# Two-layer graph network on one core: GpSimd makes the weighted one-hot columns of six of the 37 edge groups

## The chip, the cores and the metric

The kernel runs on one core of a Trainium2 chip. The metric is the device time of one execution in microseconds (us): the median of three timed runs. The engines are TensorE (PE in the profile, PEld for its weight loads), VectorE (DVE), ScalarE (ACT), GpSimd (POOL) and SyncE (SP, which here only issues DMAs).

## The reference, cut to what matters

There are N = 1250 nodes of F = 1024 features and E = 40000 edges, sorted by destination.

```python
h = jnp.maximum(_layernorm(x), 0.0)
W = jnp.zeros((1024, 1024)).at[src, dst].add(edge_weight)   # sparse weight matrix
x = x + h @ W.T + L0_bias
h = jnp.maximum(_layernorm(x), 0.0)
# two graph layers over the same edges
agg = segment_sum(h[src], dst); mean = agg / max(deg, 1)
h1 = relu(h @ W_self0 + mean @ W_neigh0 + b0)
out = x + (h1 @ W_self1 + mean(h1) @ W_neigh1 + b1)
```

Both uses of the edges are matrices that can be built once: the counts A (how many edges go from source s to destination d) and the weights W.

## The kernel before, in words

**The edge stage** builds A and W. The 40000 edges form NG = 40 groups of GC = 8 chunks with EP = 125 edges each, one edge on each partition. For each group j, VectorE makes three things in `group_rows(j)`:

- `R[:, j % 6]` (`hot_rows`, L1661): for each chunk 125x128 one-hot rows of the source's low bits, 1024 columns in bf16;
- the first part of `L[:, j % 6]` (`hot_keys`, L1668): one-hot columns of the destination, within a window of WDS[j] destinations times TN = 10 source tiles;
- the second part of `L` (`weigh`, L1676): three weighted copies of the first 8 x WDS[j] columns of the first part (the edge weight is split in three bf16 terms), so 8 chunks x 3 x 8 x WDS[j] elements a partition: 1152 for WDS[j] = 6, 1536 for 8, 1920 for 10. Both inputs and the output lie in SBUF, in bf16, one input is the first part of `L` that `hot_keys` just wrote, the other the weights `w2` spread over the columns.

WDS is 4 for groups 0 to 11, 6 for 12 to 19, 8 for 20 to 26 and 10 from 27 on. The edge stage handles groups 0 to 36 (LATE = 37); three more come later by another way. In the order of VectorE's queue a group is `hot_keys`, `hot_rows`, `weigh`; R and L are rings of six, so VectorE begins group j only after TensorE has finished group j - 6 (`s_used`).

TensorE, in `column_sums(j)` (L1275 for A, L1280 for W), waits for `s_R` and `s_L` of the group and then runs for each of the 8 chunks one matmul into A's window and three into W's. Afterwards it adds the older content of W's window (L1291), and for the next set of groups it clears a bank (L1328). Before the waits of every third group from 6 on, TensorE's sequencer reads the next 24 offsets from the table `tab_o` into registers (`load_offsets`). ScalarE evicts the sums (L1080 for A, L1087 for W).

GpSimd's queue holds constants at the start (its last is the third `affine_select` on `narrow`, L877), then waits for `s_tabd` and for `s_built`, which VectorE gives after the edge stage, and adds the windows of A (L897). After group 36 VectorE's queue continues with `h0_lo(0)` (L1655), which waits for ScalarE's `h0_hi(0)`. After group 36 TensorE turns the second tile of h and then W (L1377), and from there on goes through mixing (L1384), the block products (L1449) and the neighbour sums (L1493).

Of the kernel before, what the change touches and what calls it, by code (L numbers as in the profile page):

```python
# [10 lines left out]
ALU = mybir.AluOpType  # L11
# [8 lines left out]
TN = -(-N // NT)  # L20
# [4 lines left out]
EP = 125  # L25
GC = 8
NG = E // (EP * GC)
WD = 10
AW = 50
WW = 64  # L30
TW = F // NT
# [3 lines left out]
WDS = [4] * 12 + [6] * 8 + [8] * 7 + [WD] * 13  # L35
# [13 lines left out]
NQ = 6  # L49
# [5 lines left out]
AT_ONCE = 24  # L55
BASES = {3: range(4, 8), 8: range(8, 16), 15: range(16, 32), 31: range(32, LATE)}
TURN_STATS = 8
OV = WD
NCONST = 13
NLATER = 3 * len(set(WDS)) + 1  # L60
# [51 lines left out]
def build_program(nc, x, x_cols, dst, src_cols, dst_cols, weight_cols, L0_gnn_bias, L1_gnn_W_self0, L1_gnn_W_neigh0,  # L112
# [10 lines left out]
    with ctx:  # L123
# [3 lines left out]
        def sem(name):  # L127
            return ctx.enter_context(nc.semaphore(name))
# [68 lines left out]
        w2 = sb("w2", [EP, NG, GC, 3, 2], BF16, build)  # L197
# [5 lines left out]
        L = sb("L", [EP, NQ, GC, LS], BF16, build)  # L203
# [16 lines left out]
        q = sb("q", [P, 2, 2, PAIRS, HF], F32, products)  # L220
# [75 lines left out]
        s_ml = sem("s_ml")  # L296
# [50 lines left out]
        s_wc = sem("s_wc")  # L347
# [16 lines left out]
        s_R = sem("s_R")  # L364
        s_hot = sem("s_hot")
        s_L = sem("s_L")
        s_used = sem("s_used")
        s_asum = sem("s_asum")
        s_sum = sem("s_sum")
# [208 lines left out]
        def further_windows(eng, total, body, then=None):  # L578

            with eng.If(total > 0):  # L580
                with eng.Fori(0, NG) as b:
                    b = nc.s_assert_within(b, 0, NG - 1, skip_runtime_bounds_check_because=clamped)
                    count, less = load(eng, more[0:1, bass.ds(b, 1), :].rearrange("p b r -> p (b r)"), 0, NG * NK)
                    with eng.If(count > 0):
                        with eng.Fori(1, count + 1) as k:
                            k = nc.s_assert_within(k, 1, NK - 1, skip_runtime_bounds_check_because=clamped)
                            body(b, k, nc.s_assert_within(less + k, 1, NG * NK,
                                                          skip_runtime_bounds_check_because=clamped))
                if then is not None:
                    then()  # L590

        def twice(a, groups):
            return a.unsqueeze(3).to_broadcast([EP, groups, GC, 2])
# [226 lines left out]
        def _(pool):  # L820
# [47 lines left out]
            for wd in sorted(set(WDS)):  # L868
                a = WDS.index(wd)
# [5 lines left out]
            for tier, wd in enumerate(TIERS):  # L875
# [2 lines left out]
                                   fill=float(WD - wd), base=sum(w < wd for w in WDS), pattern=[[0, 1]],  # L878
                                   channel_multiplier=-1).then_inc(s_alone, 1)


            a_bases = []

# [104 lines left out]
        def _(act):  # L988
# [99 lines left out]
            for j in range(2 * KT):  # L1088
                if j == TURN_STATS + 2:
                    columns_and_mean(2)  # L1090
# [166 lines left out]
        def _(pe):  # L1257
# [65 lines left out]
            for j in range(LATE):  # L1323
                w = SET_OF[j]
                if j == SETS[w][0]:
                    if w >= 2:
                        pe.wait_ge(s_w, w - 1)
                    pe.matmul(w_bank(j)[:, :], none[:, 0:P], none[:, :], start=True, stop=False)  # L1328
                if j == 0:
                    pe.wait_ge(s_tabo, 16)  # L1330
                if j == 3:
                    pe.wait_ge(s_far, 1)
                    pe.transpose(furthest_turned(), furthest[:, :], ident[0:EP, 0:EP]).then_inc(s_fart, 1)
                if j == 9:
                    pe.wait_ge(s_later, NLATER)
                    pe.wait_ge(s_spread, 1)
                    row = bank[7][0:1, :]
                    pe.matmul(row[:, 0:NG], further[:, :], ident[0:NG, 0:NG], start=True, stop=True)
                    pe.matmul(row[:, NG:2 * NG], further[:, :], before[:, :], start=True, stop=True)
                    pe.matmul(general_sums(), ones[:, 0:EP], general_d[:, :], start=True, stop=True)  # L1340
                    pe.matmul(row[:, 2 * NG:2 * NG + 1], further[:, :], ones[:, 0:1], start=True, stop=True) \
                        .then_inc(s_row, 1)
                if j not in offsets_of:
                    load_offsets(j)
                if j in BASES:
                    if j == 3:
                        pe.wait_ge(s_tabw, 16)
                    base_of.update(zip(BASES[j], load(pe, tab_w[0:1, BASES[j].start:BASES[j].stop], 0, F)))
                offsets = offsets_of[j]
                pe.wait_ge(s_R, j + 1)  # L1350
                pe.wait_ge(s_L, j + 1)
                column_sums(j)
                if j == LATE - 4:
                    turn_h0(0)
# [187 lines left out]
        def _(dve):  # L1542
# [127 lines left out]
                    order.rearrange("p (n t) -> p n t", t=2).unsqueeze(1).to_broadcast([EP, GC, cols // 2, 2]),  # L1670
                    keys.unsqueeze(2).to_broadcast([EP, GC, cols // 2, 2]), ALU.is_equal)

            def weigh(q, ws, wd):

                cols = TW * wd
                return dve.tensor_tensor(  # L1676
                    L[:, q, :, TN * wd:TN * wd + 3 * cols],
                    L[:, q, :, 0:cols].unsqueeze(2).to_broadcast([EP, GC, 3, cols]),
                    ws.unsqueeze(2).to_broadcast([EP, GC * 3, cols // 2, 2]), ALU.mult)

            def group_rows(j):

                if j >= NR:
                    dve.wait_ge(s_used, j - NR + 1)
                if j == 0:
                    dve.wait_ge(s_twice, 1)
                    hot_rows(R[:, j % NR, :, :], slo2[:, j, :, :]).then_inc(s_R, 1)
                    dve.wait_ge(s_twice, 2)
                if j == FIRST:
                    dve.wait_ge(s_twice, 3)  # L1690
                if j == WDS.index(TIERS[0]):
                    dve.wait_ge(s_later, NLATER)
                hot_keys(L[:, j % NQ, :, 0:ka(j)], key2[:, j, :, :], places[WDS[j]][:, :]).then_inc(s_hot, 1)
                if j > 0:
                    hot_rows(R[:, j % NR, :, :], slo2[:, j, :, :]).then_inc(s_R, 1)
                if j == 0:
                    dve.wait_ge(s_wc, 3)
                if j == FIRST:
                    dve.wait_ge(s_wc, 4)
                dve.wait_ge(s_hot, j + 1)  # L1700
                weigh(j % NQ, w2[:, j, :, :, :].rearrange("p c r t -> p (c r) t"), WDS[j]).then_inc(s_L, 1)

            def span_of_groups(j, before):

# [58 lines left out]
            def one_more(b, k, n):  # L1763
                dve.tensor_scalar(keyw[:, :, :], key[:, bass.ds(b, 1), :].rearrange("p b c -> p (b c)")
                                  .unsqueeze(2).to_broadcast([EP, GC, 2]),
                                  skip[:, bass.ds(k, 1)], tier_of[:, bass.ds(b, 1)], ALU.subtract, ALU.add).then_inc(s_mk, 1)
                hot_rows(R[:, 0, :, :], slo2[:, bass.ds(b, 1), :, :].rearrange("p b c t -> p (b c) t"))
                dve.wait_ge(s_mk, 2 * n - 1)
                hot_keys(L[:, 0, :, 0:KA], keyw[:, :, :], places[WD][:, :]).then_inc(s_mk, 1)
                dve.wait_ge(s_mk, 2 * n)  # L1770
                weigh(0, w2[:, bass.ds(b, 1), :, :, :].rearrange("p b c r t -> p (b c r) t"), WD).then_inc(s_ml, 1)
                firsts = load(dve, tab[0:1, bass.ds(b, 1), :].rearrange("p b c -> p (b c)"), -WD, N - 1)
                dve.wait_ge(s_ms, n)
                for c in range(GC):

                    dve.reg_alu(place, firsts[c] + k * WD, N, ALU.min)
                    dve.reg_alu(place_w, firsts[c] + k * WD, F, ALU.min)
                    at = nc.s_assert_within(nc.snap(place, engines=bass.OrderedEngineSet([dve.engine])), 0, N,
                                            skip_runtime_bounds_check_because=clamped)
                    at_w = nc.s_assert_within(nc.snap(place_w, engines=bass.OrderedEngineSet([dve.engine])), 0, F,  # L1780
                                              skip_runtime_bounds_check_because=clamped)
                    dve.wait_ge(s_ma, GC * n - GC + c + 1)
                    a = ATd[:, bass.ds(at, WD), :]
                    for to, sums in ((a[:, :, 0:TW], later_sums(c, 0)[:, 0:KW]), (a[:, :, TW:TN], later_sums(c, 0)[:, KW:KA])):
                        dve.tensor_tensor(to, to, sums.rearrange("p (d s) -> p d s", d=WD), ALU.add)
                    w = Wd[:, bass.ds(at_w, WD), :]
                    dve.tensor_tensor(w, w, later_sums(c, 1).rearrange("p (d s) -> p d s", s=TW), ALU.add) \
                        .then_inc(s_ma, 1)
# [5 lines left out]
            for j in range(2 * KT):  # L1794
                if j == TURN_STATS:
                    mix_A(2)
                if j == TURN_STATS + 4:
                    for i in range(2):
# [211 lines left out]
```

## Time and profile before

| | |
|---|---|
| median of 3 runs | 805.08 us (804.27 to 805.58) |
| span of the profiled execution, first to last instruction | 802.3 us |
| busy share of the span: PE, PEld, DVE, ACT, POOL | 96%, 80%, 60%, 46%, 51% |
| the edge stage in the trace | to about 91.4 us |
| mean granted TensorE clock | 0.987 |

The profiled execution has no time of its own beside its span; the median of the runs is 2.7 us above the span, which is taken as what lies around the first and last instruction. In the profile L1661 means line 1661 of the kernel. Times of rows are microseconds from the span's start.

### The profile page before, as it was taken

To read this page: it belongs to the slowest core of one execution; us is meant where nothing else is said; L and a number is where in the kernel's file an instruction comes from. 1 tells how busy PE (TensorE), PEld (TensorE's weight loads), DVE (VectorE), ACT (ScalarE), POOL (GpSimd) and SP (SyncE) were. 2 spreads that over 40 slices of the span, in tenths; PEclk is the share of its full clock that TensorE was granted. 3 is DMA by queue.
4 is the path that set the end of the run, shared out by engine and by line. 5 is a ranking of instruction groups with operands and counts; after the bars stand their busy time and mean duration, and the time that the engine had idled before them with its cause. 6 is when DMAs were issued, how large, how long until landed. Compare 5 with 4: busy or idle time off the path is not lost.

```text
span 802.3 us, 13275 instructions
## 1 busy us (share of the span) xinstructions
PE 769.9 (96%) x4553; PEld 639.1 (80%) x4554; DVE 485.3 (60%) x720; ACT 370.8 (46%) x526; POOL 412.3 (51%) x569
## 2 busy tenths in 40 slices
PE   3878999999999999999999999999999999999998
PEld 2767888888888888888887888888888888887787
DVE  7989377777554788867413342136568766246444
ACT  7757634333364232223246886453233223347653
POOL 5000167676649899765742210127899756724311
PEclk9689999999999999999999999999999999999999
DMA  3112456775565853577855654566745659667654
GB/s 111 42 57 92 137 178 192 237 228 186 191 225 193 275 169 116 182 230 269 278 180 189 210 158 105 171 209 229 261 134 164 202 198 332 216 206 268 223 163 142
DMA packets 83239, 151.40 MB, mean 189 GB/s; under 512 B 10979, under 2 KB 21278, under 8 KB 83168
## 3 DMA queue, kind: packets, MB, share of 16 engines
q1 hardware_dynamic: 61646, 102.65, 40.8%
q10 hardware_dynamic: 20002, 42.91, 15.0%
q0 software_dynamic: 1520, 4.92, 1.5%
q8 instruction: 40, 0.66, 0.4%
q14 instruction: 31, 0.25, 0.1%
HBM read 103.79 MB, written 46.65 MB: 188 GB/s over the span
## 4 chain that ended last, share of the span: by engine, by line
PE 82%; DVE 8%; DMA 3%; POOL 3%; issue 2%; ACT 2%; POOLq 0%; SPq 0%; ACTq 0%; DVEq 0%
PE bank L1449 45%; PE bank L1493 18%; PE bank L1384 13%; DVE L L1676 2%; DVE R L1661 2%; PE bank L1280 1%; PE bank L1296 1%; DVE L L1668 1%; PE bank L1510 1%; DMA cst<-prod1g_scratch 1%; DMA b<-in_L_gnn_b 1%; PE bank L1377 1%; PE bank L1275 1%; POOL split L935 1%; ACT Ax L1160 1%
## 5 line engine op out<-in xcount | busy, mean ns | idle before, releaser
L1449 PE MATMUL bank<-slot,split 128*128 128x512 f32 x1680 | 386.3, 390 | 0.2 <-POOL split L935 0.2
L1449 PEld LDWEIGHTS bank<-slot,split 128*128 128x128 f32 x1680 | 313.7, 188 | 66.0 <-issue 1.5
L897 POOL TENSOR_TENSOR AT<-AT,az 128x50 int32 (+3 forms) x288 | 95.5, 332 | 119.7 <-DMA az<-asum_scratch 78.7
L935 POOL TENSOR_TENSOR split<-stage,split 128x512 fp32r<-128x512 f32 x50 | 66.5, 1331 | 116.9 <-ACT split L1128 116.8
L1160 ACT CAST Ax<-AT 128x1280 fp32r<-128x1280 uint16 x40 | 106.6, 2667 | 34.5 <-PE bank L1493 27.5
L1811 DVE TENSOR_TENSOR slot<-T,slot 128x512 fp32r<-128x512 f32 x64 | 90.1, 1430 | 23.8 <-ACT slot L1119 22.0
L1384 PE MATMUL bank<-slot,split_m 128*128 128x512 f32 x320 | 91.2, 396 | 0.0
L1933 DVE SCALAR_TENSOR_TENSOR cst<-bank,dinv,stage 128x512 f32<-128x512 f32 (+1 forms) x41 | 30.3, 738 | 94.8 <-PE bank L1493 94.6
L1128 ACT CAST split<-stage 128x512 fp32r<-128x512 f32 x50 | 31.1, 624 | 118.1 <-PE bank L1449 67.4
L1493 PE MATMUL bank<-slot,Ax 128*128 128x512 f32 (+1 forms) x336 | 77.6, 383 | 0.4 <-ACT Ax L1160 0.4
L952 POOL TENSOR_TENSOR T<-T,wst 128x512 f32<-128x512 f32 x48 | 69.4, 1462 | 5.2 <-DMA wst<-in_L_gnn_W_self 5.2
L1493 PEld LDWEIGHTS bank<-slot,Ax 128*128 128x128 f32 x336 | 60.3, 188 | 12.3 <-issue 0.8
L1384 PEld LDWEIGHTS bank<-slot,split_m 128*128 128x128 f32 x320 | 58.5, 188 | 11.1
L1275 PE MATMUL bank<-L,R 125*128 125x40 bf16 (+3 forms) x296 | 44.2, 203 | 18.5 <-DVE L L1676 7.9
L1811 DVE TENSOR_TENSOR slot<-wst,slot 128x512 fp32r<-128x512 f32 x48 | 44.8, 960 | 28.1 <-ACT slot L1119 28.1
L1384 PE MATMUL bank<-WTlo,split_m 128*128 128x512 f32 x160 | 49.5, 390 | 0.0
L1493 PE MATMUL bank<-g_first,Ax 128*128 128x512 f32 x200 | 48.6, 389 | 0.0
L1275 PEld LDWEIGHTS bank<-L,R 125*128 125x128 bf16 x296 | 30.5, 103 | 22.6 <-issue 11.5
L1119 ACT CAST slot<-T 128x512 fp32r<-128x512 f32 x64 | 38.6, 621 | 21.2 <-POOL T L952 14.0
L960 POOL TENSOR_TENSOR slot<-cst,slot 128x512 fp32r<-128x512 f32 x16 | 21.7, 1356 | 46.1 <-ACT slot L1175 46.1
L1280 PE MATMUL bank<-L,R 125*128 125x32 bf16 (+3 forms) x888 | 45.3, 197 | 0.0
L1280 PEld LDWEIGHTS bank<-L,R 125*128 125x128 bf16 x888 | 41.8, 104 | 3.3 <-issue 1.0
(193 smaller groups left out, 1030.6 us busy)
## 6 DMA issues: line engine op xcount, KB each, us to landing
stage<-hT_scratch SPq DMA_DIRECT2D x90, 256.0 KB, 3.6
wst<-in_L_gnn_W_neigh SPq DMA_DIRECT2D x56, 256.0 KB, 4.3
wst<-in_L_gnn_W_self SPq DMA_DIRECT2D x56, 256.0 KB, 3.3
x1b_scratch<-x ACTq DMA_DIRECT2D x10, 512.0 KB, 6.1
hT_scratch<-hTs ACTq DMA_DIRECT2D x10, 512.0 KB, 3.2
stage<-prod0s_scratch SPq DMA_DIRECT2D x20, 256.0 KB, 3.0
hT_scratch<-h1s ACTq DMA_DIRECT2D x20, 256.0 KB, 3.5
stage<-prod1s_scratch SPq DMA_DIRECT2D x20, 256.0 KB, 2.7
```

Source lines behind the costliest of these rows:

```text
L897: pool.tensor_tensor(a, a, az32[:, n % NZ, pairs * pos:pairs * (pos + 1)], ALU.add) \
L935: pool.tensor_tensor(split[:, v % 2, 1, :], source(v), split[:, v % 2, 0, :].bitcast(F32), ALU.subtract).then_inc(s_olo, 1)
L952: last = pool.tensor_tensor(T[:, b, :], T[:, b, :], wst[:, c % NS, :], ALU.subtract)
L1119: act.copy(slot[t % 2][:, 0, HF * b:HF * (b + 1)], block_source(c)).then_inc(s_whi, 1)
L1128: act.copy(split[:, v % 2, 0, :], source(v)).then_inc(s_ohi, 1)
L1160: act.copy(Ax[:, o % 2, :, :], ATd[:, NT * n:NT * (n + 1), :].rearrange("p d s -> p s d")).then_inc(s_ax, 1)
L1275: last = pe.matmul(a_bank(n)[:, at:at + ka(j)], row, L[:, q, c, 0:ka(j)], start=(c % SHARED[j] == 0), stop=ends)
L1280: last = pe.matmul(w_bank(j)[:, bass.ds(offsets[c // SHARED[j]], kw(j))], row, L[:, q, c, ka(j) + kw(j) * part:ka(j) + kw(j) * (part + 1)] ...
L1384: last = pe.matmul(bank[2 * (i % 2) + half][0:NT, :], split_m[:, i % 2, a, NT * k:NT * (k + 1)], WT[b][:, k, HF * half:HF * (half + 1)], s ...
L1449: last = pe.matmul(dense_bank(v, which)[:, :], split[:, v % 2, a, NT * k:NT * (k + 1)], slot[t % 2][:, b, HF * (HK * which + k):HF * (HK * ...
L1493: last = pe.matmul(halves_bank(rest_o, part)[:, cols], Ax[:, o % 2, s, :], g_parts(half, s)[:, b, cols], start=(s == 0 and b == 0), stop=( ...
L1811: dve.tensor_tensor(lo, block_source(c), hi.bitcast(F32), ALU.subtract).then_inc(s_wlo, 1)
```

## The change: GpSimd weighs groups 13, 17, 21, 25, 29 and 33

`weigh` becomes a function that takes the engine. VectorE no longer issues it for the six groups of `POOL_WEIGHS`. GpSimd issues it for them, each after VectorE's `hot_keys` of the same group (`s_hot`), and signals `s_Lpool`; the six stand in GpSimd's queue behind its constants and ahead of its waits for `s_tabd` and `s_built`. TensorE waits for `s_Lpool` in these groups and for a reduced count of `s_L` in the others. The sizes are two groups of 1152 elements, two of 1536 and two of 1920.

```diff
+POOL_WEIGHS = range(13, 36, 4)
+        def weigh(eng, q, ws, wd):
+            cols = TW * wd
+            return eng.tensor_tensor(
+                L[:, q, :, TN * wd:TN * wd + 3 * cols],
+                L[:, q, :, 0:cols].unsqueeze(2).to_broadcast([EP, GC, 3, cols]),
+                ws.unsqueeze(2).to_broadcast([EP, GC * 3, cols // 2, 2]), ALU.mult)
+        def weigh_group(eng, j):
+            return weigh(eng, j % NQ, w2[:, j, :, :, :].rearrange("p c r t -> p (c r) t"), WDS[j])
...
+            pool.wait_ge(s_wc, 4)
+            for j in POOL_WEIGHS:
+                pool.wait_ge(s_hot, j + 1)
+                weigh_group(pool, j).then_inc(s_Lpool, 1)
...
-                pe.wait_ge(s_L, j + 1)
+                if j in POOL_WEIGHS:
+                    pe.wait_ge(s_Lpool, POOL_WEIGHS.index(j) + 1)
+                else:
+                    pe.wait_ge(s_L, j + 1 - sum(a < j for a in POOL_WEIGHS))
...
+                if j in POOL_WEIGHS:
+                    return
                 dve.wait_ge(s_hot, j + 1)
-                weigh(j % NQ, w2[:, j, :, :, :].rearrange("p c r t -> p (c r) t"), WDS[j]).then_inc(s_L, 1)
+                weigh_group(dve, j).then_inc(s_L, 1)
```

## Rows read from the trace of the kernel before

**Rows 1.** The page: busy time by engine, and the clock in 40 slices of 20 us

```profile
PE 769.9 (96%) x4553; PEld 639.1 (80%) x4554; DVE 485.3 (60%) x720; ACT 370.8 (46%) x526; POOL 412.3 (51%) x569
...
PEclk9689999999999999999999999999999999999999
```

**Rows 2.** Timeline of DVE: start, us, engine, line, operation, [idle before <-releaser]

```profile
30.67 0.74 DVE L1676 TENSOR_TENSOR L<-L,w 125x1152 bf16<-125x1152 bf16 x1
...
44.54 0.49 DVE L1668 TENSOR_TENSOR L<-places,key 125x640 bf16<-125x640 bf16 x1 [1.33 <-PE bank L1280]
...
51.44 0.49 DVE L1668 TENSOR_TENSOR L<-places,key 125x640 bf16<-125x640 bf16 x1 [1.19 <-PE bank L1280]
...
53.62 0.49 DVE L1668 TENSOR_TENSOR L<-places,key 125x640 bf16<-125x640 bf16 x1 [0.21 <-PE bank L1280]
...
58.30 0.57 DVE L1668 TENSOR_TENSOR L<-places,key 125x800 bf16<-125x800 bf16 x1 [0.85 <-PE bank L1280]
...
71.73 0.69 DVE L1661 TENSOR_TENSOR R<-iota,slo 125x1024 bf16<-125x1024 bf16 x1
...
78.80 1.15 DVE L1676 TENSOR_TENSOR L<-L,w 125x1920 bf16<-125x1920 bf16 x1
88.23 1.29 DVE L1655 TENSOR_TENSOR split_m<-bank,split_m 128x512 fp32r<-128x512 f32 x2 [8.28 <-ACT split_m L1036]
```

**Rows 3.** Timeline of PE: the first matmul of groups 13, 27, 33 and 36

```profile
37.67 0.26 PE L1275 MATMUL bank<-L,R 125*128 125x60 bf16 x1
...
69.19 0.20 PE L1275 MATMUL bank<-L,R 125*128 125x100 bf16 x1 [1.42 <-DVE L L1676]
...
82.17 0.20 PE L1275 MATMUL bank<-L,R 125*128 125x100 bf16 x1 [1.20 <-issue]
...
88.30 0.21 PE L1275 MATMUL bank<-L,R 125*128 125x100 bf16 x1
```

**Rows 4.** PE's waits from 35 to 90: us in total, times, longest

```profile
PE bank L1275 <- DVE R L1661: 5.6, 4, 2.1
PE bank L1275 <- DVE L L1676: 3.8, 3, 1.4
```

**Rows 5.** Tile tab_o from 66 to 70: duration in ns min/median/max, first and last start

```profile
L498 PEldq TENSOR_LOAD <-tab_o x1: 2030/2030/2030, 67.0 to 67.0; - x1
```

**Rows 6.** Groups of DVE by shape, weigh alone: busy us, mean ns

```profile
L1676 DVE TENSOR_TENSOR L<-L,w 125x1920 bf16<-125x1920 bf16 x10 | 11.5, 1152 | 0.0
L1676 DVE TENSOR_TENSOR L<-L,w 125x1536 bf16<-125x1536 bf16 x7 | 6.7, 951 | 0.0
...
L1676 DVE TENSOR_TENSOR L<-L,w 125x1152 bf16<-125x1152 bf16 x8 | 5.9, 742 | 0.0
```

**Rows 7.** Single lines over the whole span: duration in ns min/median/max

```profile
L897 POOL TENSOR_TENSOR AT<-AT,az x288: 214/256/1354, 95.1 to 260.3; 128x50 int32 x52, 128x20 int32 x32, 128x30 int32 x32, 128x40 int32 x28
...
L1811 DVE TENSOR_TENSOR slot<-T,slot x64: 676/1558/1778, 250.9 to 644.4; 128x512 fp32r<-128x512 f32 x64
```

**Rows 8.** Timeline of DVE and POOL from 307 to 311

```profile
307.43 1.67 DVE L1811 TENSOR_TENSOR slot<-T,slot 128x512 fp32r<-128x512 f32 x1
...
309.03 1.78 DVE L1811 TENSOR_TENSOR slot<-T,slot 128x512 fp32r<-128x512 f32 x1
...
307.26 1.29 POOL L921 TENSOR_TENSOR S<-S,stage 128x512 f32<-128x512 f32 x1
...
308.51 1.75 POOL L952 TENSOR_TENSOR T<-T,wst 128x512 f32<-128x512 f32 x1
```

**Rows 9.** POOL's groups by shape from 0 to 20: busy us, mean ns

```profile
L849 POOL MEMSET none<- 125x512 bf16 x1 | 0.5, 519 | 0.0
L823 POOL MEMSET ident<- 128x128 f32 x1 | 0.2, 203 | 0.0
```

**Rows 10.** L877, POOL's last constants: all three, and the second in the timeline

```profile
L877 POOL TENSOR_SCALAR_AFFINE_SELECT narrow<-narrow x3: 178/1445/2924, 13.6 to 18.1; 40x1 f32<-40x1 f32 x3
...
15.14 2.92 POOL L877 TENSOR_SCALAR_AFFINE_SELECT narrow<-narrow 40x1 f32<-40x1 f32 x1
```

More of the change, by code:

```diff
@@ L366, in build_program @@
         s_L = sem("s_L")
+        s_Lpool = sem("s_Lpool")
         s_used = sem("s_used")
@@ L1671, in hot_keys @@
                     keys.unsqueeze(2).to_broadcast([EP, GC, cols // 2, 2]), ALU.is_equal)
[L1673 to L1679, printed above, removed]
             def group_rows(j):
@@ L1770, in one_more @@
                 dve.wait_ge(s_mk, 2 * n)
-                weigh(0, w2[:, bass.ds(b, 1), :, :, :].rearrange("p b c r t -> p (b c r) t"), WD).then_inc(s_ml, 1)
+                weigh(dve, 0, w2[:, bass.ds(b, 1), :, :, :].rearrange("p b c r t -> p (b c r) t"), WD).then_inc(s_ml, 1)
                 firsts = load(dve, tab[0:1, bass.ds(b, 1), :].rearrange("p b c -> p (b c)"), -WD, N - 1)
```

## The prediction

> **What bounds the kernel now.** I read the page first. TensorE is busy for 96% of the span and DVE for 60% [rows 1]: over the whole kernel TensorE sets the time, so a change in the edge stage is worth what it does to the moment at which TensorE leaves that stage. From about 91 us on TensorE hardly waits, so I carry a delay or a gain at that point one to one to the end.
>
> Then I read the two timelines of the stage side by side, to see who is ahead. DVE ends group 13's weigh at 30.67 + 0.74 = 31.4 [rows 2], and TensorE begins that group at 37.67 [rows 3]: DVE is 6.3 us ahead. It ends group 36 at 78.80 + 1.15 = 79.95 [rows 2], TensorE begins it at 88.30 [rows 3]: 8.35 us ahead. Between them DVE is so far ahead that it meets the end of its ring: four times it waits for TensorE to free a slot, 1.33 + 1.19 + 0.21 + 0.85 = 3.58 us in all, the last before group 27 at 58.30. After that it runs without a gap to 79.95, and then idles 8.28 us until ScalarE gives it h0's tile [rows 2]. So DVE does not bound this stage from group 13 on; it has 3.58 + 8.35 = 11.9 us to spare.
>
> The table of waits seems to say otherwise: TensorE's first matmul of a group waits 5.6 + 3.8 = 9.4 us at seven places, and the row names DVE [rows 4]. I don't believe the name. These waits stand before every third group, for example 1.42 us before group 27 at 69.19 [rows 3], and there TensorE's sequencer is reading its offset table from 67.0 to 69.03 [rows 5]; group 27's columns, begun at 58.30 and ended some 2.2 us later [rows 2], had been ready for 8.6 us. This is the case in which the named engine had long been done.
>
> **What the change removes.** Six weighs leave DVE: two each of 0.742, 0.951 and 1.152 us [rows 6], 5.69 us. Consecutive DVE instructions overlap by some 0.07 us, so DVE gets 5.3 us back. As DVE is not the bound, that alone moves the end by nothing: the cover is TensorE's own work and its table reads.
>
> **What it adds on GpSimd.** The trace has no bf16 tensor_tensor on GpSimd, so its price is bounded from neighbours. Undisturbed adds take 214 ns for the smallest, 20 elements [rows 7], and 1.29 us for 512 in f32 [rows 8]: (1290 - 214) / 492 = 2.19 ns an element over a foot of 0.17 us. A lower bound is half of that, if two bf16 elements went as one; the nearest row on this is the fill, (519 - 98) / 511 = 0.82 ns in bf16 beside (203 - 98) / 127 = 0.83 ns in f32 with the foot of about 98 ns that the one-column fills show [rows 9]: the type makes no difference there. I take 2.19. An upper bound of 3 ns stands for the cost of a broadcast pattern and of rounding, an estimate without a row. So the weighs take 2.7, 3.5 and 4.4 us, against the 6.3 us and more by which the columns are early. GpSimd has nothing else to do here, and its next work waits for DVE's signal after the stage. By itself this is hidden as well.
>
> **What it adds on DVE.** All three operations of DVE in a group read two SBUF tensors, and so does the new GpSimd one. What two such streams do to each other stands at 307 us [rows 8]: GpSimd runs 307.26 to 308.55 undisturbed, and DVE's operation begun at 307.43 needs 1.67 us where it needs 0.676 alone [rows 7]; it is held until GpSimd is done. The next GpSimd operation, begun at 308.51, takes 1.75 us: it waits for DVE's, which ends at 309.10. DVE's second, from 309.03, takes 1.78. They take turns by whole instructions. The longest DVE one is 1.778 - 0.676 = 1.10 us over the shortest [rows 7], for 512 GpSimd elements: 2.15 ns an element for which DVE stands still. (The Trainium skill, page "SBUF — State Buffer", section "Who interferes with whom", says that a VectorE instruction with two SBUF inputs and a GpSimd instruction that reads SBUF exclude each other for a whole instruction, and that whoever issues first gets the ports; rows 8 agree with it, and rows 10 below don't fit it. By it the sum is the one below. It is the rule that speaks against this change.)
>
> So each moved weigh stops DVE for 1152, 1536 or 1920 times 2.15 ns = 2.48, 3.30 or 4.13 us. R of the same group is not hit: `hot_rows` follows `hot_keys` at once, before GpSimd has the signal. GpSimd takes the ports when `hot_rows` ends, and the next group's `hot_keys` is what stands. Behind it stands all of DVE's queue, and for its results TensorE waits.
>
> **The sum.**
> - Six stops: 2 x (2.48 + 3.30 + 4.13) = 19.8 us.
> - Less the weighs no longer done: 5.3. DVE is 14.5 us later at group 36.
> - Less the four ring waits, which vanish as DVE falls back: 3.58. All four lie before group 27, and by then four of the stops have come (11.6 less 3.1 us, so 8.5): they are used up whole. 10.9 remain.
> - Less the lead at group 36, 8.35: about 2.6 us late.
>
> Check at group 33, where it should first show: its `hot_rows` started at 71.73 [rows 2] and would now start 8.5 - 3.6 + 3.1 = 8.0 later and end at 80.3; GpSimd ends 4.4 us on, at 84.7. TensorE would have begun at 82.17 [rows 3]: 2.5 us late. Both ways give the same.
>
> The profiled span of 802.3 becomes about 804.9; the 2.7 us between span and median stay. Median 805.08 + 2.6 = 807.7 us. 0.2% of this kernel, 1.6 us, is about what its measurement can tell from no change; the forecast is a little above it. It is zero if DVE stands less than 17.2 us in all (1.87 ns an element), and passes 1.6 us at 2.04 ns.
>
> **The rivals.**
>
> *Hidden.* The stops are shorter than 2.04 ns an element (faster bf16, or the ports held for part of the operation): the margins eat everything, 805.1 us. For it: the smaller end of the price is 1.1 ns. Against: fills show no gain of bf16 [rows 9] and the 1.10 us are measured. At 1.1 ns the stops are 10.1 us, DVE is 4.8 later, less than its 11.9.
>
> *Dearer weigh.* At 2.6 ns an element the stops are 24.0 us, 6.8 late: 811.9; at 3 ns 10.4 late. For it: the moved operation multiplies with two broadcast patterns in bf16, which no row shows. A stop of TensorE could also cost it its clock (the second slice of 20 us is at 0.6, and group 13's matmul took 0.26 us against 0.20 for a wider one later [rows 1, 3]); that would add 1 to 2 us.
>
> *GpSimd starves.* L877's second operation works on 40x1 elements, takes 178 ns when nothing is beside it, and lasted from 15.14 to 18.06, to the end of a run of back-to-back two-input DVE operations [rows 10]; DVE was not slowed. If the weighs behave so, each starts only when DVE stands at the end of its ring. Then group 25's runs when DVE has filled the ring to 30, and group 33's when it has filled it to 36, at about 86; with 4.4 us it ends at 90.2 where TensorE would begin at 82.17: 8 us late, 813 us. Against: tensor_tensor took its turn between two DVE operations in rows 8.
>
> *Faster.* If the 9.4 us of rows 4 were truly waits for DVE, its six shorter groups would come earlier by up to 5.3 us: 799.8 us. It decides only if DVE is the last that TensorE waits for, which the lead of 6 to 8 us contradicts, and if the stops are under the weighs they replace, 0.65 ns an element.
>
> **How the numbers follow.** Forecast 0.38 (of it 0.10 within 1.6 us), hidden 0.27, dearer 0.17, starving 0.12, faster 0.06. Slower 0.28 + 0.17 + 0.12 = 0.57, same 0.37, faster 0.06. The predicted time is the forecast's, 807.7. The range reaches down over the hidden case to 804.0 and up over the dearer one to 812.5; outside are the faster case and half of the two dear ones' upper parts. The forecast's own range is 806.3 to 809.5.
>
> **What would show it.** GpSimd's L rows from about 30 to 86 us, 2.7 to 4.4 us plus a wait of up to 0.7 for `hot_rows`; DVE's `hot_keys` of groups 14, 18, ... 34 lengthened by 2.4 to 4.1 us; no DVE waits for TensorE at 44 to 58; TensorE's waits before group 33, new and some 2.5 us beyond 82.17, and its turn of W beginning near 94. `hot_keys` at their old length with GpSimd lasting 10 us would mean starving; GpSimd under 1.9 ns an element would mean hidden. The prediction is wrong if DVE runs on beside GpSimd, or if TensorE's table reads were not what it waited for.

## The result, and the profile after

The median of the changed kernel is 812.41 us (811.33 to 813.62, 4 runs) beside 804.73 us for the kernel before (804.27 to 805.58, 4 runs): a ratio of 1.0098, 95% interval 1.0082 to 1.0114. It is 7.7 us slower where 2.6 us were forecast. The time lies just inside the stated range, but at three times the forecast step. The profiled execution took 811.46 us, its span is 809.7 us, 7.4 us over that of before.

The page of the changed kernel, busy time and the granted clock in 40 slices; the first row answers to the first of [rows 1]:

```profile
PE 771.6 (95%) x4553; PEld 639.7 (79%) x4554; DVE 489.8 (60%) x714; ACT 370.7 (46%) x526; POOL 445.3 (55%) x575
...
PEclk9989899999999999999999999999999999999999
```

DVE has lost its six weighs (720 to 714 instructions) and is still busier, 489.8 against 485.3 us: the records of five of its operations now contain the time for which they are held, 10.6 us in all. GpSimd has gained 33 us for six operations of which the costliest was priced at 4.4.

The six new operations in the timeline of POOL, changed kernel (groups 13, 17, 21, 25, 29, 33 in this order):

```profile
30.25 4.02 POOL L597 TENSOR_TENSOR L<-L,w 125x1152 bf16<-125x1152 bf16 x1 [11.98 <-DVE L L1688]
...
37.79 10.43 POOL L597 TENSOR_TENSOR L<-L,w 125x1152 bf16<-125x1152 bf16 x1 [3.52 <-DVE L L1688]
...
48.18 2.75 POOL L597 TENSOR_TENSOR L<-L,w 125x1536 bf16<-125x1536 bf16 x1
...
55.53 3.14 POOL L597 TENSOR_TENSOR L<-L,w 125x1536 bf16<-125x1536 bf16 x1 [4.60 <-DVE L L1688]
...
65.37 11.34 POOL L597 TENSOR_TENSOR L<-L,w 125x1920 bf16<-125x1920 bf16 x1 [6.70 <-DVE L L1688]
...
76.67 3.73 POOL L597 TENSOR_TENSOR L<-L,w 125x1920 bf16<-125x1920 bf16 x1
```

Two operations of one size, 1152 elements, last 4.02 and 10.43 us; two of 1920 last 11.34 and 3.73. So size does not set them. What does stands beside them in the timeline of DVE (L1688 is `hot_keys`, L1681 `hot_rows`, L597 the weigh), answering to [rows 2]:

```profile
32.60 1.93 DVE L1688 TENSOR_TENSOR L<-places,key 125x480 bf16<-125x480 bf16 x1
...
45.30 0.95 DVE L597 TENSOR_TENSOR L<-L,w 125x1536 bf16<-125x1536 bf16 x1
49.96 1.33 DVE L1688 TENSOR_TENSOR L<-places,key 125x640 bf16<-125x640 bf16 x1 [3.71 <-PE bank L1297]
...
56.47 2.55 DVE L1688 TENSOR_TENSOR L<-places,key 125x640 bf16<-125x640 bf16 x1 [0.42 <-PE bank L1297]
...
72.77 0.68 DVE L1681 TENSOR_TENSOR R<-iota,slo 125x1024 bf16<-125x1024 bf16 x1
73.59 3.55 DVE L1688 TENSOR_TENSOR L<-places,key 125x800 bf16<-125x800 bf16 x1
77.06 3.88 DVE L1681 TENSOR_TENSOR R<-iota,slo 125x1024 bf16<-125x1024 bf16 x1
```

Group 17's weigh, ready from 37.79, ends at 48.22. DVE runs back to back to 45.30 + 0.95 = 46.25 and then stands, because its ring is full; 48.22 is 1.97 us after that. Group 29's, ready from 65.37, ends at 76.71; DVE's run ends at 72.77 + 0.68 = 73.45, and 3.26 us later the weigh is done. DVE's next operation, begun in the gap of 0.14 us, is held until GpSimd is through (3.55 us for a `hot_keys` of 0.57). The others fell on a gap or soon after one: group 13's on four short operations without a second SBUF input before 32.60, group 21's on the wait of 3.71 us, group 25's on that of 0.42 us, and group 33's right behind group 29's, one held `hot_keys` later. Once it is let in, GpSimd needs 1.97 us for 1152 elements and 3.26 for 1920: 1.7 ns an element.

What TensorE makes of that, the first matmuls of groups 17, 29, 30, 31, 33 and 36 (the last two answer to [rows 3], 82.17 and 88.30):

```profile
48.32 0.21 PE L1292 MATMUL bank<-L,R 125*128 125x60 bf16 x1 [3.46 <-issue]
...
76.85 0.20 PE L1292 MATMUL bank<-L,R 125*128 125x100 bf16 x1 [2.82 <-POOL L L597]
...
79.89 0.24 PE L1292 MATMUL bank<-L,R 125*128 125x100 bf16 x1 [0.74 <-issue]
...
83.08 0.29 PE L1292 MATMUL bank<-L,R 125*128 125x100 bf16 x1
...
88.85 0.20 PE L1292 MATMUL bank<-L,R 125*128 125x100 bf16 x1 [1.20 <-issue]
...
94.99 0.20 PE L1292 MATMUL bank<-L,R 125*128 125x100 bf16 x1
```

Groups 17 and 29 begin 0.10 and 0.14 us after GpSimd's ends of 48.22 and 76.71. Ahead of group 17 TensorE stands for 3.46 us. The name "issue" in that row hides GpSimd: the start follows GpSimd's end. Group 17 began at 46.52 before, so it is only 1.8 us late, and 1.1 of them are left at group 28 (72.14 against 71.00). These differences are smaller than the stop because the two executions were not alike ahead of it, as one window of each shows (columns: busy us, instructions, granted clock, DMA share, GB/s; before, then changed):

```profile
36.00:40.00 4.00, 4.00 (x86) 0.55 0.25 74
```

```profile
36.00:40.00 4.00, 3.47 (x86) 1.00 0.25 75
```

By that the changed kernel had been 1.0 us ahead at group 15 (41.84 against 42.87). Group 29 began at 72.74 before: 4.1 us late. Group 33 is 6.7 late although its weigh was ready at 80.4, and from there the distance stays (94.99 against 88.30). The 2.6 us between groups 29 and 33 are TensorE's clock, in the windows of PE of the changed kernel:

```profile
76.00:80.00 4.00, 2.40 (x36) 0.79 0.19 64
80.00:84.00 4.00, 4.00 (x48) 0.50 0.19 64
84.00:88.00 4.00, 3.65 (x61) 0.86 0.20 68
```

Before, all windows from 72 to 92 show 1.00, this one among them:

```profile
80.00:84.00 4.00, 2.81 (x53) 1.00 0.21 68
```

After the stop ahead of group 29 the clock is at its lower level, 1.2 GHz, for some 7 us, and matmuls last 0.29 in place of 0.21 us. From group 36 to the end the changed kernel takes 714.7 us against 714.0. That difference is no more than executions differ by: e7_distance, where TensorE waited for no GpSimd operation in the edge stage, takes 717.2.

### The profile page after: what moved, and what is told of

The parts are those of the page before. It is cut to its first block, busy times and chain, and to the rows that moved or that the text cites. A ratio compares the mean times of both kernels' runs of the same rounds, so it can differ in the third digit from the quotient of the medians.

```text
span 809.7 us, 13276 instructions
## 1 busy us (share of the span) xinstructions
PE 771.6 (95%) x4553; PEld 639.7 (79%) x4554; DVE 489.8 (60%) x714; ACT 370.7 (46%) x526; POOL 445.3 (55%) x575
## 4 chain that ended last, share of the span: by engine, by line
PE 82%; DVE 7%; POOL 4%; DMA 2%; issue 2%; ACT 2%; POOLq 0%; SPq 0%; ACTq 0%; DVEq 0%
PE bank L1469 44%; PE bank L1513 19%; PE bank L1404 13%; DVE L L597 1%; POOL L L597 1%; DVE R L1681 1%; DVE L L1688 1%; PE bank L1297 1%; PE bank L1313 1%; PE bank L1530 1%; DMA cst<-prod1g_scratch 1%; ACT Ax L1177 1%; PE bank L1397 1%; POOL split L952 1%; PE bank L1292 1%
## 5 line engine op out<-in xcount | busy, mean ns | idle before, releaser
L914 POOL TENSOR_TENSOR AT<-AT,az 128x50 int32 (+3 forms) x288 | 93.8, 326 | 68.3 <-DMA az<-asum_scratch 24.1
L1292 PEld LDWEIGHTS bank<-L,R 125*128 125x128 bf16 x296 | 30.6, 103 | 29.1 <-issue 20.5
L597 POOL TENSOR_TENSOR L<-L,w 125x1152 bf16<-125x1152 bf16 (+2 forms) x6 | 35.3, 5900 | 26.8 <-DVE L L1688 26.8
```

Of the source, the lines that this page charges most:

```text
L597: return eng.tensor_tensor(L[:, q, :, TN * wd:TN * wd + 3 * cols], L[:, q, :, 0:cols].unsqueeze(2).to_broadcast([EP, GC, 3, cols]), ws.uns ...
L914: pool.tensor_tensor(a, a, az32[:, n % NZ, pairs * pos:pairs * (pos + 1)], ALU.add) \
L1292: last = pe.matmul(a_bank(n)[:, at:at + ka(j)], row, L[:, q, c, 0:ka(j)], start=(c % SHARED[j] == 0), stop=ends)
```

## The experiments

In each experiment the second time, after "beside", is the median of the kernel before, run along with it.

### e1_stand: VectorE waits while GpSimd weighs

```diff
                 if j in POOL_WEIGHS:
+                    dve.wait_ge(s_Lpool, POOL_WEIGHS.index(j) + 1)
                     return
```

> The change, with one wait more: after hot_rows of each of the six groups VectorE waits until GpSimd's weigh of that group is done. Three theories. GAPS (GpSimd's operation gets the shared ports only when VectorE's back-to-back two-input operations leave a gap, and by itself takes about 1.7 ns an element): the gap is now there at once, so GpSimd's operations last 2.0, 2.6 and 3.3 us (plus at most the 0.6 us of hot_rows), VectorE stands 2 x 7.8 = 15.7 us less 5.3 saved = 10.4, which is under its 11.9 us of slack, and the time is that of the kernel before, 804.7 (803.5 to 806). DEAR (the bf16 operation with broadcast patterns is itself slow, 4 to 11 us): VectorE stands 2 x (4 + 5 + 10) us or more, and the time is above 815. TURNS (the recorded forecast, 2.15 ns an element whoever waits): 807.3, as recorded.

Measured: 805.63 us beside 805.86, ratio 1.0004 (0.9991 to 1.0016). Three of DVE's six waits, one of each size:

```profile
32.99 0.41 DVE L1688 TENSOR_TENSOR L<-places,key 125x480 bf16<-125x480 bf16 x1 [2.02 <-POOL L L597]
...
49.96 0.49 DVE L1688 TENSOR_TENSOR L<-places,key 125x640 bf16<-125x640 bf16 x1 [2.65 <-POOL L L597]
...
80.92 0.57 DVE L1688 TENSOR_TENSOR L<-places,key 125x800 bf16<-125x800 bf16 x1 [3.29 <-POOL L L597]
```

An added wait takes the loss away, to within 1.3 us. DVE stands 2 x (2.02 + 2.65 + 3.29) = 15.9 us, saves 5.3, and the 10.6 fit in the 11.9 of slack, though only just. Ahead of group 33, where a table read alone cost 1.20 us before [rows 3], TensorE now waits for GpSimd:

```profile
81.03 0.20 PE L1292 MATMUL bank<-L,R 125*128 125x100 bf16 x1 [1.68 <-POOL L L597]
```

That makes TensorE 0.5 us later. DVE's last weigh ends at 87.49, and TensorE begins group 36 at 87.63. GpSimd's operation is not dear: DEAR has fallen. It only has to be let in.

### e2_beside and e6_beside_again: the same six operations, on a scratch tile that TensorE doesn't read

```diff
+            pool.wait_ge(s_hot, j + 1)
+            pool.tensor_tensor(probe[...], probe[...] (8 x 3 x cols), probe[...] (24 x cols/2 x 2), ALU.mult)
...
+            dve.wait_ge(s_probe, 7)                           # e2 alone, ahead of h0_lo(0)
```

> The kernel before (VectorE makes all weighs, no engine waits for GpSimd's), plus six GpSimd operations of the weigh's shape, type and patterns on a scratch tile, started by the same signals of the same six groups. It takes the dependence of TensorE away and keeps the meeting at the ports. GAPS: GpSimd's records last 3 to 12 us where VectorE runs back to back, VectorE is held only where it had a gap anyway, TensorE never waits: 804.5 to 806.5. TURNS: every GpSimd operation stops VectorE for 2.0 to 4.1 us, 15.7 to 19.8 in all against 11.9 of slack, so 808.5 to 812.6, with hot_keys of the next group lengthened each time. DEAR: GpSimd's records are equally long in a gap and without one.

Measured: 810.22 us beside 805.86, ratio 1.0050 (1.0036 to 1.0063), outside of what GAPS gave. The trace shows the cause in the experiment itself: at the end of its stage DVE had to wait for the last of the six.

```profile
91.81 1.29 DVE L1677 TENSOR_TENSOR split_m<-bank,split_m 128x512 fp32r<-128x512 f32 x2 [6.77 <-POOL probe L902]
```

That operation began at 88.23 before [rows 2]. TensorE was not late up to there: it began group 36 at 87.13. So e6_beside_again puts the scratch tile into `wst`, where VectorE has no wait for it and only SyncE waits, before it loads the first blocks there.

> As e2_beside, but the scratch tile lies where it is written again only after 100 us, so VectorE has no wait for the six operations at the end of its stage (in e2_beside that wait made h0_lo(0) begin at 91.8 us instead of 88.2, by itself 3.6 us). GAPS: with no engine waiting for GpSimd, what is left is what the ports cost, and GpSimd gets them mostly where VectorE stands anyway: 804.5 to 806. TURNS: 15.7 us of stops against 11.9 of slack: 808.5 or more. If the 4 us of e2_beside were the ports' and not that wait's, this run stays at 809 to 811.

Measured: 804.74 us beside 804.75, ratio 1.0003 (0.9986 to 1.0021). With TensorE and VectorE waiting for none of the six, nothing is lost. The run says little of what holding VectorE costs: GpSimd was let in only once during VectorE's stage, at group 13, and held one `hot_keys` for 1.5 us; the last four ran after the stage. GpSimd's operations of groups 17, 21 and 29 in its timeline, and DVE in one window:

```profile
38.45 40.96 POOL L890 TENSOR_TENSOR wst<-wst 125x1152 bf16<-125x1152 bf16 x1 [3.59 <-DVE L L1690]
79.49 2.76 POOL L893 TENSOR_TENSOR wst<-wst 125x1536 bf16<-125x1536 bf16 x1
...
85.17 3.41 POOL L899 TENSOR_TENSOR wst<-wst 125x1920 bf16<-125x1920 bf16 x1
```

```profile
38.50:76.40 37.90, 37.90 (x59) 0.93 0.23 76
```

One GpSimd operation stood for 40.96 us behind 59 DVE operations that follow each other without a gap, and began when they ended. Alone it takes (3.41 - 2.76) / 384 = 1.69 ns an element over 0.17 us.

### e3_forms, e7_distance and e12_three_apart: who gets a turn, and when

```diff
+            pool.wait_ge(s_hot, j + 1)                        # e3: j = 15, 28, 30, 32
+            pool.tensor_tensor(probe, probe, probe)           # bf16 128x512, f32 128x512, f32 125x512, bf16 128x512
```

> The kernel before, plus four GpSimd operations on a scratch tile inside stretches in which VectorE runs two-input bf16 operations back to back: bf16 multiply 128x512 at group 15, f32 add 128x512 at group 28, f32 add 125x512 at group 30, bf16 add 128x512 at group 32. It asks what makes a GpSimd operation take its turn (as at 307 us in the kernel before) or wait for a gap (as L877 there, and the weighs of the change). If it is VectorE's stream alone: all four last until VectorE's next gap, several us each, 28's until VectorE stops. If it is the 16-bit type: the f32 ones last 1.3 to 2.0 us and lengthen one VectorE operation by 1.1, the bf16 ones wait for a gap. If it is the partition count: only the one on 125 waits. If it is the broadcast pattern: none waits.

GpSimd's operations at groups 15 (bf16), 28 (f32) and 32 (bf16), in its timeline:

```profile
34.48 10.33 POOL L887 TENSOR_TENSOR probe<-probe 128x512 bf16<-128x512 bf16 x1 [13.03 <-DVE L L1684]
...
59.57 1.58 POOL L890 TENSOR_TENSOR probe<-probe 128x512 f32<-128x512 f32 x1 [14.77 <-DVE L L1684]
...
70.34 1.48 POOL L896 TENSOR_TENSOR probe<-probe 128x512 bf16<-128x512 bf16 x1 [3.80 <-DVE L L1684]
```

The one at group 30, f32 on 125 partitions, took 1.59. None of the four readings holds: a plain bf16 operation of one size waits 10 us at group 15 (multiply) and takes its turn at group 32 (add). A single execution took 804.62 us.

> The kernel before with three GpSimd operations on scratch: f32 add 128x512 at group 15, the weigh's bf16 pattern with 1920 elements at group 28, f32 add 128x512 at group 34. In e3_forms and e2_beside operations got their turn between two VectorE operations when VectorE had stood or been held 1.4 to 2.9 us earlier, and waited for a gap when it had last stood 3.3 us or more before; kind and distance were mixed there. KIND (f32 or plain operations get a turn, the weigh does not): both f32 ones last 1.3 to 2 us and lengthen a VectorE operation by 1.1, the one at 28 lasts over 10 us. DISTANCE (what matters is how long VectorE has run without a pause): the f32 ones at 15 and 34 last until the next gap (5 to 10 us), the weigh at 28, some 3 us after VectorE's last ring wait, gets its turn and lasts about 3.7 us.

```profile
33.80 10.48 POOL L887 TENSOR_TENSOR wst<-wst 128x512 f32<-128x512 f32 x1 [14.66 <-DVE L L1681]
...
61.15 3.72 POOL L890 TENSOR_TENSOR wst<-wst 125x1920 bf16<-125x1920 bf16 x1 [16.87 <-DVE L L1681]
...
77.30 6.97 POOL L893 TENSOR_TENSOR wst<-wst 128x512 f32<-128x512 f32 x1 [12.43 <-DVE L L1681]
```

KIND has fallen: f32 waits at 15 and 34, and the weigh itself, broadcast patterns, bf16 and 1920 elements, gets its turn at 28 between two DVE operations. A single execution took 807.25 us, within the 802.14 to 807.54 of the kernel before run along with it, with TensorE at group 36 at 88.34, as before.

> The kernel before with a GpSimd f32 add 128x512 on scratch at group 28 and another at group 31. In e3_forms operations two groups apart (28, 30, 32) each got their turn, five VectorE instructions and 2.8 us after VectorE had last been held. Here the second comes eight instructions and 4.9 us after. DISTANCE: 28's lasts 1.6 us, 31's until VectorE ends its stage near 80 us. KIND or chance: both last 1.6 us.

```profile
59.15 1.57 POOL L887 TENSOR_TENSOR wst<-wst 128x512 f32<-128x512 f32 x1 [39.86 <-DVE L L1678]
66.67 13.43 POOL L890 TENSOR_TENSOR wst<-wst 128x512 f32<-128x512 f32 x1 [5.96 <-DVE L L1678]
```

DISTANCE holds (a single execution, 803.95 us). In the timeline of DVE its last wait before group 28, and the weigh that GpSimd's turn holds up (1.15 us otherwise):

```profile
56.26 0.57 DVE L1678 TENSOR_TENSOR L<-places,key 125x800 bf16<-125x800 bf16 x1 [0.36 <-PE bank L1290]
...
59.51 2.22 DVE L1686 TENSOR_TENSOR L<-L,w 125x1920 bf16<-125x1920 bf16 x1
```

The same operation takes its turn five DVE operations and 2.9 us after DVE last stood. At group 31, eight operations and 4.9 us after the hold, it stands until the end of DVE's stage. With group 17 of the change (seven operations and 3.3 us after a hold, starved) the border lies between five and seven operations, or between 2.9 and 3.3 us. Which of the two counts, and why, stays open.

### e8_nudge: a gap without a wait

```diff
                 if j in POOL_WEIGHS:
+                    dve.memset(wst[:, 0, 0:256], 0.0)
                     return
```

> The change, with a short VectorE memset of 128x256 f32 (about 0.3 us, no SBUF input) after hot_rows of each of the six groups, and no wait added. GAPS: one operation without a second SBUF input is gap enough, GpSimd's weighs start there and last 2.3 to 3.9 us by their records, hot_keys of the next group is held 1.7 to 3.2 us, and the time is 804 to 806 as with e1_stand; VectorE loses 0.3 us x 6 more than there. If a gap must be a true standstill, GpSimd's weighs last 10 us as in the change and the time is above 811.

Measured: 805.21 us beside 804.75, ratio 1.0007 (0.9990 to 1.0024). DVE at groups 13 and 33:

```profile
30.64 0.27 DVE L1713 MEMSET wst<- 128x256 f32 x1
30.84 0.33 DVE L1688 TENSOR_TENSOR L<-places,key 125x480 bf16<-125x480 bf16 x1
...
76.23 0.27 DVE L1713 MEMSET wst<- 128x256 f32 x1
76.43 3.49 DVE L1688 TENSOR_TENSOR L<-places,key 125x800 bf16<-125x800 bf16 x1
```

At group 33 GpSimd slips in during a memset of 0.27 us and holds the next `hot_keys` for 2.9 us, and so it does at groups 17, 21, 25 and 29. Its six operations last 2.50 to 4.23 us. A single operation without a second SBUF input was gap enough in these five cases. At group 13 it was not: GpSimd's operation, there from 30.18, didn't hold the `hot_keys` behind the memset and ended at 34.41, which is 1.97 us after 32.44, so it was again let in by the four short operations from 32.36 on. In the kernel before, too, a `tensor_reduce` of 0.14 us at 16.58 did not let in the 40x1 operation of [rows 10]. What sets the two cases apart stays open.

### e4_last_two and e5_first_four: parts of the change

```diff
-POOL_WEIGHS = range(13, 36, 4)
+POOL_WEIGHS = range(29, 36, 4)      # e4; e5: range(13, 28, 4)
```

> The change for groups 29 and 33 alone. GAPS: VectorE has no gap from 58.3 on until it meets the end of its ring, so group 29's weigh is late by 1 to 3 us and TensorE's clock may drop behind that stop: 806 to 811, most of the loss of the full change. TURNS: two stops of 3.3 to 4.1 us less 2.1 saved, at most 6.1, are under the 8.35 us of lead: 804.7, no change.

> The change for groups 13, 17, 21 and 25 alone. GAPS: group 17's weigh again waits for VectorE to meet the end of its ring, TensorE begins that group 1 to 2 us late, and part of it is made good before group 27 as in the full change (1.8 us late at group 17, 1.15 at group 27): 805 to 807. TURNS (stops of 2.15 ns an element, 11.6 less 3.1 us saved = 8.5, under 11.9 of slack): no change. DEAR: above 815. Together with the run of groups 29 and 33 it shows whether the full change is the sum of its parts, 1.0098.

Measured: e4 808.68 beside 805.86, ratio 1.0040 (1.0024 to 1.0056); e5 810.82 beside 804.75, ratio 1.0060 (1.0037 to 1.0084), more than expected. TensorE's late group in e4, and the one after it; and in e5:

```profile
83.26 0.20 PE L1292 MATMUL bank<-L,R 125*128 125x100 bf16 x1 [3.03 <-POOL L L597]
...
87.53 0.20 PE L1292 MATMUL bank<-L,R 125*128 125x100 bf16 x1
```

```profile
68.72 0.22 PE L1292 MATMUL bank<-L,R 125*128 125x80 bf16 x1 [5.17 <-POOL L L597]
```

In both it is another group than in the full change. In e4 group 29 falls on a ring wait of 0.72 us and 33 is starved, 3.03 us of wait; the next group follows after 4.27 us in place of 2.67, and the window 84 to 88 has a clock of 0.61. In e5 group 17 falls on a ring wait and loses nothing, while 25 stands for 13.64 us and costs 5.2. The two losses add up to 1.0%, as the change's own does, but they don't lie at the same places: that sum is no proof of anything.

### e10_stand_twelve: the sum at its other side

```diff
-POOL_WEIGHS = range(13, 36, 4)
+POOL_WEIGHS = range(13, 36, 2)      # on top of e1_stand
```

> e1_stand with twelve groups instead of six: 13, 15, ... 35. VectorE waits for each of GpSimd's weighs, so none waits for a gap. It tests the sum of the prediction at its other side. By the sum with 1.70 ns an element: stops 4 x 1.96 + 3 x 2.61 + 5 x 3.26 = 32.0 us, plus about 0.1 us of signal each (1.2), less saved weighs 4 x 0.67 + 3 x 0.87 + 5 x 1.07 = 10.6, less 11.9 of slack: TensorE leaves the stage 10.7 us late, 815.4 (813.5 to 817.5). If the slack is worth less or the stops cost more, it is slower than that; if VectorE does not bound the stage even then, 804.7.

Measured: 816.77 us beside 804.61, ratio 1.0162 (1.0138 to 1.0187), 12 to 13 us where 10.7 were expected. The sum has the right size; the rest was not taken apart. TensorE waits 9.1 us for GpSimd at six places, the longest 2.6, and begins group 36 at 99.12. One part of the loss is again the clock after a stop of TensorE (2.39 us, ahead of group 33), window of PE of this kernel:

```profile
92.00:96.00 4.00, 4.00 (x44) 0.60 0.19 64
```

### e9_small_reads: what TensorE waits for before every third group

```diff
-AT_ONCE = 24
+AT_ONCE = 8
```

> The kernel before with one number changed: TensorE's sequencer reads its offsets for one group at a time (8 values) instead of for three groups (24 values). It asks what the waits of 1.2 to 1.4 us before every third group are, which the page puts down to VectorE. READS (TensorE's engine runs dry while its sequencer reads, 1.76 us in the median for 24 values; its queued matmuls cover about 0.5 us of it): reads of 8 values last some 0.5 to 0.7 us and are covered, most of the eight waits of 1.2 to 1.4 us go, TensorE comes up to VectorE and the kernel gets up to 9 us faster, 796 to 803. VECTORE (the page's name is right): the waits stay where they are and the time is 804.7.

Measured: 800.15 us beside 804.61, ratio 0.9947 (0.9931 to 0.9962): this version beats both kernels. Tile tab_o over the whole span, and PE's waits from 35 to 90, answering to [rows 5] and [rows 4]:

```profile
L498 PEldq TENSOR_LOAD <-tab_o x35: 534/592/1936, 10.6 to 81.8; - x35
```

```profile
PE bank L1275 <- ACT asum L1080: 1.5, 2, 1.3
...
PE bank L1275 <- DVE R L1661: 0.3, 1, 0.3
```

The waits that the table of before put down to DVE, 9.4 us, were reads of the offset table. Cut into pieces of 0.59 us in place of 1.76 in the median they are hidden, and 0.3 us with DVE's name is left, beside 1.5 with ScalarE's and 0.6 without a name. TensorE begins group 36 at 82.61, 5.7 us earlier; the time gains 4.5.

### e11_change_small_reads: the change on top of it

The edit is that of e9_small_reads, made in the changed kernel.

> The change on top of e9_small_reads (offsets read for one group at a time). There VectorE met the end of its ring nowhere, and led by 6.6 us at group 36. GAPS: TensorE gives VectorE fewer ring waits, so GpSimd gets the ports later still: group 17's weigh comes when VectorE stands before group 23, near 46.5 us, 3 to 4 us late for TensorE; group 25's when it stands before group 31, another 4 to 5; over e9_small_reads' 800.2 that is 5 to 11 us more, 805 to 811. TURNS or holds alone (10.4 us net against 6.6 of lead): 804.

Measured: 811.35 us beside 804.97, ratio 1.0079 (1.0050 to 1.0107). Over e9_small_reads that is 1.0079 / 0.9947 = 1.0133, some 10.7 us, in the expected range of the difference at its upper end; the time itself lies 0.35 us above the expected 811. Group 17 is again starved (TensorE begins it at 48.39 against 45.05), and then 29, not 25:

```profile
65.02 13.49 POOL L597 TENSOR_TENSOR L<-L,w 125x1920 bf16<-125x1920 bf16 x1 [6.70 <-DVE L L1688]
```

So the starved weigh stands longer here than in the change, 13.49 against 11.34 us. Whether the change also costs more here is not shown: from the two intervals I estimate 1.010 to 1.017 for it, and the change alone has 1.0082 to 1.0114.

## Why the prediction was wrong, point by point

**What bounds the stage: right.** DVE has slack, and the waits with its name were table reads (e9_small_reads: 9.4 us become 0.3). The faster rival had its condition there and fell with it. (Its border of 0.65 ns an element is 0.58 by its own numbers, 5.3 us over 9216 elements.)

**The price on GpSimd: over-sized.** 2.19 ns an element was taken from f32; the bf16 multiply takes 1.69 over the same foot of 0.17 us (e6_beside_again). With broadcast patterns and all, it is cheaper than the plain f32 add. The dearer rival has fallen as to its price, whose bound of 3 ns no run shows; that a stop of TensorE would cost it its clock, 1 to 2 us, stood there too and came true with 2.6.

**The stops of DVE: over-sized.** With 2.02, 2.65 and 3.29 us (e1_stand) they sum to 15.9 us and not 19.8. By the prediction's own sum that is 10.6 net against 11.9 of slack, below its stated border of 17.2 us: hidden. In e1_stand and e8_nudge, where GpSimd is let in by a wait or a memset, the time is that of before. (In e8_nudge it is let in at once in five of six cases.) So this mechanism alone, rightly sized, made no difference that these runs can tell; the 2.6 us that it forecast are not there.

**The slack: taken from one execution.** The 3.58 us of ring waits came where TensorE was slow, at a granted clock of 0.50 to 0.55 from 28 to 40 us. In e6_beside_again, with a clock of 1.00 up to 36 us, DVE meets the end of its ring nowhere, its lead at group 36 is 8.0 us and one hold took 1.5 of it, so the slack was 9.5 us and not 11.9. That six stops of 10.6 us net stay hidden is therefore a narrow matter: in e1_stand TensorE was some 0.5 us late at group 33 for them.

**The step that failed** is "GpSimd takes the ports when `hot_rows` ends". The prediction took from [rows 8] that two streams take turns by whole instructions. In these runs they do so only shortly after DVE has stood or been held; in [rows 8] DVE's operation was held by GpSimd itself, so the case was always of that kind. In a longer back-to-back run of DVE GpSimd gets nothing, whatever its operation (e7_distance, e12_three_apart). In the place of a stop behind each `hot_rows` came holds at other places, 10.6 us in all, and two late weighs, group 17's and 29's: TensorE stood 3.46 and 2.82 us for them, and behind the second its clock cost 2.6 us more.

**The rival "GpSimd starves"** was this, priced at 8 us late and given 0.12; measured were 7.7. That the two numbers are so close is luck. Its row, the 40x1 operation of 2.92 us in [rows 10], was read rightly and weighed against too few rows: it and [rows 8] don't contradict each other. Its walk was right in kind, though not in place: it made groups 25 and 33 late, and it left out the clock. That the measured time lies inside the stated range is luck as well, for its upper part was meant for the dearer rival.

**How the loss adds up.** Between the two profiled executions 1.1 us are left at group 28, 3.0 come with group 29 and 2.6 with the clock behind it. The last two are read within the stage and are firm. The first is not: in six executions in which TensorE never waited for GpSimd (before, e2, e3, e6, e7, e12) group 28 begins between 68.00 and 71.00 and group 36 between 85.41 and 88.34, and the one that the change is compared with is at the late end or next to it. Against the others the change is up to 9.6 us late at group 36. The 7.7 us of the medians stand; their split is known to about 3 us.

**The rule of the Trainium skill** ("SBUF — State Buffer", "Who interferes with whom") that whoever issues first gets the ports for a whole instruction holds for the hold, 2.99 us of a `hot_keys` at 73.59. It does not describe who comes next: in e6_beside_again a waiting GpSimd operation was passed over by 59 of VectorE's. The measurement decides: who is there first does not always come next.

## What to carry to other kernels

Before two-input work moves from VectorE to GpSimd, look at how long VectorE runs two-SBUF-input operations back to back. GpSimd's operation may not begin before that run ends, so its price is its own time plus the rest of the run. A wait of VectorE for it let it in each time (e1_stand), a memset of 0.3 us in five cases of six (e8_nudge). And an engine named in a table of waits should be checked against when its result was ready: here the true cause, register reads of the sequencer, was worth 0.5%, and one changed number of the kernel gained it.

## What the runs showed of the hardware that was not expected

- A GpSimd tensor_tensor that reads SBUF stood for 40.96 us behind 59 VectorE operations (e6_beside_again), and got its turn between two of them five operations after VectorE had last stood (e12_three_apart). Type, form and 125 or 128 partitions did not decide it (e3_forms, e7_distance).
- On GpSimd the bf16 multiply takes 1.69 ns an element over 0.17 us (e6_beside_again), the f32 add of 512 elements 1.29 us in all ([rows 8]).
- A stop of TensorE of 2.8 us was followed by some 7 us at the lower clock (0.50 in the window 80 to 84), which cost about as much as the stop: 2.6 us. In e4_last_two a stop of 3.03 us cost 1.6 us more behind it. The clock also falls without such a stop: to 0.50 from 28 to 36 us in the kernel before.
